# Router logits computed with the rows as matmul weights, the batch term put into the accumulator first, and the first rows and gate columns loaded and split in four slices by depth

## The chip, the cores and the metric

The kernel runs on one core of a Trainium2 chip. The metric is the device time of one execution in microseconds. The time before is the median of three runs.

The engines are TensorE (PE in the rows; its weight loads are shown apart as PEld), VectorE (DVE), ScalarE (ACT), GpSimd (POOL) and SyncE (SP). Each works through its own list of instructions in order and waits on semaphores; SyncE, ScalarE and GpSimd also issue DMA transfers. Products are summed in PSUM, which TensorE writes and VectorE and ScalarE read. All else lies in SBUF, with 128 partitions.

## What is computed

Two blocks over x of 32 batches x 128 rows x 512. The change touches the first part of the first block alone: a shared gated feed-forward and the router of eight routed experts. Cut to that:

```python
x_flat = x.reshape(N, C)                                   # N = 4096, C = 512
shared_out = einsum('nh,dh->nd', silu(x_flat @ sw1.T) * (x_flat @ sw3.T), sw2)   # 1024 hidden units
t_bias = t_emb @ router_t_w.T                              # one row of 8 per batch
s = sigmoid(x_flat @ router_w.T + t_bias_flat)             # N x 8
_, topk_idx = top_k(s + router_bias, 2)
...
```

The two best experts of each row then get gates, the routed experts run, a second feed-forward picks one expert for each batch, and the second block routes rows by a hash of their token and ends in a recurrence over 32 steps. None of that is changed.

## The kernel before

The program runs five stages one after the other: `stage_shared`, `stage_routed`, `stage_ffn`, `stage_hashed` and `stage_recurrent`. Most products are done in three parts: an operand is rounded to `float32r` (`_hi`, by ScalarE) and its remainder taken (`_lo`, by VectorE), and `product` (lines 95 to 101) issues hi x hi, lo x hi and hi x lo into one accumulator. The router logits are the exception: they are plain float32 matmuls, since they decide which experts are chosen.

`stage_shared` takes the 4096 rows in G = 8 groups of TG = 4 tiles of 128 rows, with the depth of 512 in DC = 4 slices of 128. For each group `gate_up(g, first, last)` makes HC = 8 chunks of 128 hidden units: 12 products for the gate, 12 for up, each with 128x128 weights and 512 columns (the rows of the group). ScalarE applies silu, VectorE multiplies (`hidden`), and `down(g)` makes the output.

The opening loads much at once. SyncE issues `x_raw`, the rows of group 0 transposed (1 MB, also the first half of `x_grp`), then four quarters of the weights, by `COLUMNS`: half 0 or 1 of the hidden units, layer 0 (gate) or 1 (up), 1 MB each. They land in buffers borrowed from others (`w_raw`, the second half of `x_grp`, `sg_h`). ScalarE first issues eleven small constants, then rounds x (`x_hi`, line 343) and each quarter (`split_columns`, line 354) as they land. VectorE follows with the remainders (`x_lo`, line 451, and line 457). TensorE waits for the last remainder that a chunk needs.

The router runs between the chunks of group 0. `score_t(g)` (line 730) makes the logits of one group turned round: weights `r_w[:, k]` of 8 columns, moving operand 512 columns of x, four float32 matmuls into an 8x512 accumulator. VectorE adds the batch term (`add_bias`, line 470) into `logits_sb`. `turn_scores(g)` (line 737) transposes the four tiles of 8x128 into `lg_ps`, whose layout is rows x experts x tiles. The batch term itself is made first of all (line 800). When the last group is there, ScalarE applies the sigmoid (line 374) behind the sixth chunk's silu, and VectorE starts its long chain: `choose`, `gates`, `slots`, `places`.

SyncE loads the rows of the later groups for the scores (`score_x`) into the two halves of `x_grp` in turn, a group ahead. A hash ranking also needs TensorE twice in this time, into `aux_ps` (lines 806 and 811): the product of ones with the memberships of the hashed experts, and that of a triangle with them, which waits until VectorE has copied the totals of the first (`hash_totals`, line 492). On VectorE `rank_weights` (line 511 on) makes small matrices for later ranks in `last_col` and others.

## Time and profile before

| | us |
|---|---|
| median of three runs | 2581.2 |
| lowest and highest | 2580.53, 2584.6 |
| profiled execution, its time | 2581.59 |
| its span in the trace | 2579.9 |
| mean granted clock of TensorE over the span | 0.986 |

The times of the rows are from the start of the span. Timeline rows give the start, the duration, the engine, the line, the operation, output <- inputs with their shapes, and in brackets how long the engine had stood idle and what ended that. A MATMUL row has a duration that includes its way through the array; successive products overlap, so the distance between two starts tells the pace. A float32 matmul stands in the rows as two MATMUL and two LDWEIGHTS entries. The granted clock is given as a share of the full 2.4 GHz. The first stretch of the page's table of slices has PE at 8 tenths and the next two at 9; what stands below about the opening comes from the timeline.

### The profile page before, as it was taken

To read this page: it belongs to the slowest core of one execution; us is meant where nothing else is said; L and a number is where in the kernel's file an instruction comes from. 1 tells how busy PE (TensorE), PEld (TensorE's weight loads), DVE (VectorE), ACT (ScalarE), POOL (GpSimd) and SP (SyncE) were. 2 spreads that over 40 slices of the span, in tenths; PEclk is the share of its full clock that TensorE was granted. 3 is DMA by queue.
4 is the path that set the end of the run, shared out by engine and by line. 5 is a ranking of instruction groups with operands and counts; after the bars stand their busy time and mean duration, and the time that the engine had idled before them with its cause. 6 is when DMAs were issued, how large, how long until landed. Compare 5 with 4: busy or idle time off the path is not lost. (4 is left out here: it accounts for less than half of the span.)

```text
span 2579.9 us, 40827 instructions
## 1 busy us (share of the span) xinstructions
PE 2482.1 (96%) x12552; PEld 2057.4 (80%) x12553; DVE 1146.0 (44%) x1756; ACT 901.3 (35%) x1446; POOL 552.3 (21%) x493
## 2 busy tenths in 40 slices
PE   8999999998989799999999989999989999999999
PEld 4778888887878578878888869989978888888876
DVE  5655555344422234434344346667643332333356
ACT  2233333235544312222222236666542222222233
POOL 1100000002222256657666610000001111111000
PEclk9999999999999899999999989999999999999999
DMA  7698898126474343363335356666641111111035
GB/s 288 216 338 308 304 329 314 71 110 208 139 267 137 108 156 109 114 252 108 118 104 190 98 194 237 230 230 228 230 153 33 33 33 29 29 33 33 16 107 170
DMA packets 134081, 413.05 MB, mean 160 GB/s; under 512 B 30082, under 2 KB 32578, under 8 KB 117872
## 3 DMA queue, kind: packets, MB, share of 16 engines
q1 hardware_dynamic: 106912, 317.61, 34.8%
q0 software_dynamic: 18736, 60.80, 7.8%
q10 hardware_dynamic: 8352, 33.60, 3.4%
q8 instruction: 46, 0.75, 0.1%
q14 instruction: 35, 0.29, 0.0%
HBM read 558.71 MB, written 144.80 MB: 273 GB/s over the span
## 5 line engine op out<-in xcount | busy, mean ns | idle before, releaser
L99 PE MATMUL s_g<-wx_hi,s_x_hi 128*128 128x512 f32 x512 | 207.0, 404 | 8.7 <-DVE s_x_lo L2093 4.2
L101 PE MATMUL s_g<-wx_hi,s_x_lo 128*128 128x512 f32 x512 | 202.0, 395 | 0.0
L100 PE MATMUL s_g<-wx_lo,s_x_hi 128*128 128x512 f32 x512 | 201.4, 393 | 0.0
L1840 DVE TENSOR_TENSOR s_w_lo<-s_w_raw,s_w_hi 128x1024 fp32r<-128x1024 f32 x124 | 146.5, 1223 | 76.3 <-ACT s_w_hi L1769 74.6
L99 PE MATMUL s_g<-s_u,s_c_hi 128*128 128x512 f32 x384 | 152.7, 398 | 1.6 <-PEq L1656 1.6
L101 PE MATMUL s_g<-s_u,s_c_lo 128*128 128x512 f32 x384 | 149.9, 390 | 0.0
L100 PE MATMUL s_g<-s_u,s_c_hi 128*128 128x512 f32 x384 | 149.5, 389 | 0.0
L99 PE MATMUL s_h_ps<-s_x_hi,s_w_hi 128*128 128x256 f32 x512 | 146.0, 285 | 1.5 <-DVE s_x_lo L1865 1.5
L100 PE MATMUL s_h_ps<-s_x_lo,s_w_hi 128*128 128x256 f32 x512 | 145.8, 285 | 0.0
L101 PE MATMUL s_h_ps<-s_x_hi,s_w_lo 128*128 128x256 f32 x512 | 145.8, 285 | 0.0
L2021 POOL DMA_INDIRECT s_y<-mid_hash_out,first_rec x32 | 31.7, 989 | 476.7 <-DMA mid_hash_out<-s_o 394.3
L99 PEld LDWEIGHTS s_g<-wx_hi,s_x_hi 128*128 128x128 f32 x512 | 97.2, 190 | 37.7 <-issue 9.2
L2104 DVE TENSOR_TENSOR s_gate<-s_g,s_bias 128x512 f32<-128x512 f32 x96 | 66.1, 691 | 136.9 <-PE s_g L101 136.9
L1769 ACT ACTIVATE s_w_hi<-s_w_raw 128x1024 fp32r<-128x1024 f32 x124 | 124.2, 1054 | 6.1 <-DMA s_w_raw<-in_w2h 6.1
L380 ACT ACTIVATE s_sg_h<-s_gate 128x512 f32<-128x512 f32 x64 | 38.4, 599 | 249.3 <-PE s_up L101 249.3
L2027 POOL TENSOR_TENSOR s_x<-s_y,s_r 128x512 f32<-128x512 f32 x32 | 44.2, 1381 | 365.6 <-ACT s_r L2039 355.5
L2051 ACT ACTIVATE s_gate<-s_gate 128x512 f32<-128x512 f32 x96 | 60.8, 634 | 176.0 <-DVE s_gate L2104 176.0
L634 DVE TENSOR_TENSOR s_sg_h<-s_sg_h,s_up 128x512 f32<-128x512 f32 x64 | 44.0, 688 | 170.0 <-ACT s_sg_h L380 169.8
L101 PEld LDWEIGHTS s_g<-wx_hi,s_x_lo 128*128 128x128 f32 x512 | 97.0, 190 | 21.5
L970 POOL DMA_INDIRECT s_x<-in_x_rows,route x68 | 67.0, 985 | 216.8 <-PE s_tx L1180 214.2
L99 PE MATMUL s_h_ps<-s_half,s_y_hi 128*128 x256 | 105.4, 412 | 7.1 <-DMA s_half<-mid_w 5.6
L100 PEld LDWEIGHTS s_g<-wx_lo,s_x_hi 128*128 128x128 f32 x512 | 97.2, 190 | 18.9
(372 smaller groups left out, 6778.9 us busy)
## 6 DMA issues: line engine op xcount, KB each, us to landing
s_half<-mid_w ACTq DMA_DIRECT2D x124, 2048.0 KB
s_half<-mid_w SPq DMA_DIRECT2D x20, 2048.0 KB
s_w_raw<-in_w SPq DMA_DIRECT2D x64, 512.0 KB, 6.2
mid_w<-s_x_grp SPq DMA_DIRECT2D x32, 1024.0 KB, 5.4
mid_w<-s_pool_b SPq DMA_DIRECT2D x32, 1024.0 KB, 4.9
s_w_raw<-in_w1h SPq DMA_DIRECT2D x16, 2048.0 KB, 7.5
s_w_raw<-in_w2h SPq DMA_DIRECT2D x16, 2048.0 KB, 7.5
mid_routed<-s_o_sb SPq DMA_DIRECT2D x72, 256.0 KB
```

Of the source, the lines that this page charges most:

```text
L99: pe.matmul(out, a_hi, w_hi, start=first, stop=False, skip_group_check=True)
L100: pe.matmul(out, a_hi, w_lo, start=False, stop=False, skip_group_check=True)
L101: return pe.matmul(out, a_lo, w_hi, start=False, stop=last, skip_group_check=True)
L380: act.activation(sg[:, c % 2], gate_ps[c % banks][:], ACT.Silu).then_inc(S["silu"], 1)
L634: dve.tensor_tensor(h[:, c % 2], sg[:, c % 2], up_ps[c % banks][:], ALU.mult).then_inc(S["hmul"], 1)
L970: pool.indirect_dma_start(x[:, i % NI], None, ins["x_rows"], bass.IndirectOffsetOnAxis(idx[:, i:i + 1].bitcast(U32), 0)).then_inc(E[f"tile ...
L1769: act.activation(hi[:, c], raw[:, c], ACT.Copy).then_inc(S[name + "_hi"], 1)
L1840: dve.tensor_tensor(lo[:, c], raw[:, c], hi[:, c], ALU.subtract).then_inc(S[name + "_lo"], 1)
L2021: pool.indirect_dma_start(y[:], None, d["hash_out"], bass.IndirectOffsetOnAxis(rec[:, SLOTH:SLOTH + 1].bitcast(U32), 0)).then_inc(S["y_in" ...
L2027: pool.tensor_tensor(x2[:], y[:], r[:], ALU.mult).then_inc(S["x2"], 1)
L2051: act.activation(gate[:, g], gate[:, g], f).then_inc(S["acted"], 1)
L2104: dve.tensor_tensor(gate[:, g], g_ps[n][g][:], bias[:, g], ALU.add).then_inc(S["added"], 1)
```

## The change

Four things are done.

1. **First slices.** x of group 0 and the first half of the gate weights are loaded as four slices each, by depth k: x slice, weight slice, x slice, and so on, each of 256 KB with a semaphore of its own. ScalarE and VectorE split them slice by slice (`split_first`). TensorE's first work is `first_chunks(2)`: the gate products of chunks 0 and 1, then their up products. In the first chunk it waits slice by slice.
2. **Constants.** Six of the eleven constants, those of the hash and the later ones, are issued by GpSimd instead of ScalarE.
3. **Logits.** `score(g)` uses each tile of x, 128x128, as the weights and `r_w[:, k]`, 8 columns, as the moving operand, and sums straight into `lg_ps`: 16 float32 matmuls a group. The transposes, `add_bias`, `logits_sb` and the two accumulators are gone.
4. **Batch term.** VectorE multiplies `rt_w` with `cond_t` for all depths, experts and batches (`bias_terms`, 1024 elements for each partition, in the buffer of `o_sb`). Four float32 matmuls with a matrix of ones as weights sum them over the partitions into `lg_ps`, before all scores. The ones lie in `last_col`, so `rank_weights` waits for the first scores.

The other changed numbers are semaphore counts that follow from this.

```diff
+        bias_terms = o_sb[:].rearrange("p a n -> p (a n)").rearrange("p (k e i) -> p k e i", k=DC, e=ER)
+        ones_32 = last_col
...
-            sp.dma_start(x_raw, ins["xt_groups"][0]).then_inc(S["xt_in"], 16)
-            for half, layer in COLUMNS:
+            for k in range(DC):
+                sp.dma_start(x_raw[:, :, k], ins["xt_groups"][0][:, :, k]).then_inc(S[f"first_x{k}"], 16)
+                sp.dma_start(columns[0][0][:, k], ins["sw"][k, :, 0:D]).then_inc(S[f"first_w{k}"], 16)
+            for half, layer in COLUMNS[1:]:
                 units = slice(layer * DC, (layer + 1) * DC)
                 if half and layer:
-                    sp.wait_ge(S["w_lo"], 2)
+                    sp.wait_ge(S["w_lo"], DC)
...
-                    sp.wait_ge(S["xt_lo"], 1)
-                wait_for(sp, S["logits_t"], g - 1)
+                    sp.wait_ge(S["xt_lo"], DC)
+                wait_for(sp, S["logits"], g - 1)
...
+            for dst, src, name in ((ids[:], ins["ids"], "hash_const"),
+                                   (expert_no, ins["c_expert"], "hash_const"), (new_run, ins["c_run"], "hash_const"),
+                                   (tile_no[:], ins["c_tile"], "late_const"), (token_no[:], ins["c_token"], "late_const"),
+                                   (r_bias[:], ins["r_bias"].partition_broadcast(P), "late_const")):
+                pool.dma_start(dst, src).then_inc(S[name], 16)
...
-                                   (ident[:], ins["c_ident"], "const"), (ids[:], ins["ids"], "hash_const"),
-                                   (expert_no, ins["c_expert"], "hash_const"), (new_run, ins["c_run"], "hash_const"),
-                                   (tile_no[:], ins["c_tile"], "late_const"), (token_no[:], ins["c_token"], "late_const"),
-                                   (r_bias[:], ins["r_bias"].partition_broadcast(P), "late_const")):
+                                   (ident[:], ins["c_ident"], "const")):
...
+            def split_first(k):
+                act.wait_ge(S[f"first_x{k}"], 16)
+                act.activation(xt_hi[:, :, k], x_raw[:, :, k], ACT.Copy).then_inc(S["xt_hi"], 1)
+                act.wait_ge(S[f"first_w{k}"], 16)
+                act.activation(w_hi[:, k, 0:D], columns[0][0][:, k], ACT.Copy).then_inc(S["w_hi"], 1)
...
-            x_hi(0)
-            for half, layer in COLUMNS:
+            for k in range(DC):
+                split_first(k)
+            for half, layer in COLUMNS[1:]:
...
+            def split_first(k):
+                dve.wait_ge(S["xt_hi"], k + 1)
+                dve.tensor_tensor(xt_lo[:, :, k], x_raw[:, :, k], xt_hi[:, :, k], ALU.subtract).then_inc(S["xt_lo"], 1)
+                dve.wait_ge(S["w_hi"], k + 1)
+                dve.tensor_tensor(w_lo[:, k, 0:D], columns[0][0][:, k], w_hi[:, k, 0:D], ALU.subtract).then_inc(S["w_lo"], 1)
...
-            def add_bias(g):
-                dve.wait_ge(S["logits_t"], g + 1)
-                wait_for(dve, S["logits"], g - 1)
-                dve.tensor_tensor(logits_sb[:, g % 2], score_ps[g % 2][0:ER],
-                                  batch_bias[:, g * TG:(g + 1) * TG, None].to_broadcast([ER, TG, P]),
-                                  ALU.add).then_inc(S["logits_sum"], 1)
...
                 last = ident[:, P - 1:P]
+                dve.wait_ge(S["logits"], 1)
                 op(dve.memset(last_col[:], 0.0))
...
-            x_lo(0)
-            split_columns(0, 0)
+            for k in range(DC):
+                split_first(k)
             split_columns(0, 1)
             dve.wait_ge(S["const"], 16 * n_const)
+            dve.memset(ones_32[:], 1.0).then_inc(S["bias_terms"], 1)
+            dve.tensor_tensor(bias_terms, rt_w[:, :, :, None].to_broadcast([P, DC, ER, NB]),
+                              cond_t[:, :, None, :].to_broadcast([P, DC, ER, NB]), ALU.mult).then_inc(S["bias_terms"], 1)
             dve.memset(ones[:], 1.0).then_inc(S["ones"], 1)
             dve.memset(ones_f[:], 1.0).then_inc(S["ones"], 1)
             dve.tensor_copy(tri[:], tri_f[:]).then_inc(S["ones"], 1)
-            dve.wait_ge(S["bias_ps"], 1)
-            signal(dve.tensor_copy(batch_bias[:], bias_ps), "bias")
-            add_bias(0)
             split_columns(1, 0)
             hash_members()
...
-            def score_t(g):
-                if g == 0:
-                    pe.wait_ge(S["xt_in"], 16)
-                else:
+            def bias_logits():
+                pe.wait_ge(S["bias_terms"], 2)
+                for k in range(DC):
+                    pe.matmul(lg_ps, ones_32[:], bias_terms[:, k], start=(k == 0), stop=False, skip_group_check=True)
+
+            def score(g):
+                if g:
                     pe.wait_ge(S[f"x_in{g % 2}"], (g + 1) // 2 * 16)
-                wait_for(pe, S["logits_sum"], g - 1)
-                for k in range(DC):
-                    mm = pe.matmul(score_ps[g % 2][0:ER], r_w[:, k], x_grp[:, g % 2, :, k], start=(k == 0),
-                                   stop=(k == DC - 1))
-                mm.then_inc(S["logits_t"], 1)
-
-            def turn_scores(g):
-                pe.wait_ge(S["logits_sum"], g + 1)
                 for tt in range(TG):
-                    mm = pe.transpose(lg_ps[:, :, g * TG + tt], logits_sb[:, g % 2, tt], ident[0:ER, 0:ER])
+                    for k in range(DC):
+                        mm = pe.matmul(lg_ps[:, :, g * TG + tt], x_grp[:, g % 2, tt, k], r_w[:, k], start=False,
+                                       stop=(k == DC - 1), skip_group_check=True)
                 mm.then_inc(S["logits"], 1)
+
+            def first_chunks(last):
+
+                for layer, outs in enumerate((gate_ps, up_ps)):
+                    if layer:
+                        pe.wait_ge(S["w_lo"], DC + 2)
+                    for c in range(last):
+                        for k in range(DC):
+                            if layer == 0 and c == 0:
+                                pe.wait_ge(S["xt_lo"], k + 1)
+                                pe.wait_ge(S["w_lo"], k + 1)
+                            w = slice(c * P, (c + 1) * P)
+                            u = layer * DC + k
+                            mm = product(pe, outs[c][:], (w_hi[:, u, w], w_lo[:, u, w]),
+                                         (xt_hi[:, :, k], xt_lo[:, :, k]), k == 0, k == DC - 1)
+                        if layer:
+                            mm.then_inc(S["gu"], 1)
...
+            first_chunks(NG0)
             pe.wait_ge(S["const"], 16 * n_const)
-            for k in range(DC):
-                mm = pe.matmul(bias_ps, rt_w[:, k], cond_t[:, k], start=(k == 0), stop=(k == DC - 1))
-            mm.then_inc(S["bias_ps"], 1)
-            score_t(0)
-            gate_up(0, 0, 1)
+            bias_logits()
+            score(0)
             pe.wait_ge(S["ones"], 3)
             pe.wait_ge(S["hash_members"], 1)
             pe.matmul(aux_ps[:, :], ones[:], flat, start=True, stop=True).then_inc(S["pe_rank"], 1)
-            gate_up(0, 1, 2)
-            score_t(1)
-            turn_scores(0)
+            score(1)
             pe.wait_ge(S["hash_total_read"], 1)
             pe.matmul(aux_ps[:, :], tri[:], flat, start=True, stop=True).then_inc(S["pe_rank"], 1)
             for c in range(2, 5):
                 gate_up(0, c, c + 1)
-                score_t(2 * c - 2)
-                turn_scores(2 * c - 3)
-                score_t(2 * c - 1)
-                turn_scores(2 * c - 2)
+                score(2 * c - 2)
+                score(2 * c - 1)
             gate_up(0, 5, 6)
-            turn_scores(G - 1)
             gate_up(0, 6, HC)
```

TensorE, between the second and the third chunk of group 0. `L730` is a score product (in the changed kernel `L735`), `L728` the batch term's sum, `s_first` holds `lg_ps`, `s_aux` the hash ranking. Before, with the end of chunk 1:

```order
L99 MATMUL s_up<-s_xt_hi,s_w_hi 128x512
L100 MATMUL s_up<-s_xt_lo,s_w_hi 128x512
L101 MATMUL s_up<-s_xt_hi,s_w_lo 128x512
L730 MATMUL s_up<-s_x_grp,s_r_w 8x512 x4
L737 MATMUL s_first<-ident,s_o_sb 128x8 x4
L811 MATMUL s_aux<-s_member,s_tri 128x512
L99 MATMUL s_gate<-s_xt_hi,s_w_hi 128x512
```

After:

```order
L99 MATMUL s_up<-s_xt_hi,s_w_hi 128x512
L100 MATMUL s_up<-s_xt_lo,s_w_hi 128x512
L101 MATMUL s_up<-s_xt_hi,s_w_lo 128x512
L728 MATMUL s_first<-s_o_sb,s_last_col 128x256 x4
L735 MATMUL s_first<-s_r_w,s_x_grp 128x8 x16
L820 MATMUL s_aux<-s_member,s_ones 128x512
L735 MATMUL s_first<-s_r_w,s_x_grp 128x8 x16
L823 MATMUL s_aux<-s_member,s_tri 128x512
L99 MATMUL s_gate<-s_xt_hi,s_w_hi 128x512
```

The scores of groups 0 and 1 and the batch term now stand together behind chunk 1; the ones product, which stood between chunk 0 and 1, follows the scores of group 0, and the transposes are gone.

VectorE, from its start to the first hash step. Line 451 is the remainder of x, line 457 that of the weights; in the changed kernel 464, 466 and 472. Before:

```order
L451 TENSOR_TENSOR s_xt_lo<-s_x_grp,s_xt_hi 128x2048 [waits s1_xt_hi]
L457 TENSOR_TENSOR s_w_lo<-s_w_raw,s_w_hi 128x2x512 [waits s1_w_hi] x2
L457 TENSOR_TENSOR s_w_lo<-s_x_grp,s_w_hi 128x2x512 [waits s1_w_hi] x2
L644 MEMSET s_ones 128x128 [waits s1_const]
L645 MEMSET s_ones_f 128x8
L646 CAST s_tri<-s_tri_f 128x128
L648 COPY s_batch_bias<-s_first 8x32 [waits s1_bias_ps]
L470 TENSOR_TENSOR s_o_sb<-s_gate,s_batch_bias 8x512 [waits s1_logits_t,s1_bias]
L457 TENSOR_TENSOR s_w_lo<-s_sg_h,s_w_hi 128x2x512 [waits s1_w_hi] x2
L481 TENSOR_SCALAR s_hash_id<-s_ids 128x32 [waits s1_hash_const]
```

After:

```order
L464 TENSOR_TENSOR s_xt_lo<-s_x_grp,s_xt_hi 128x4x128 [waits s1_xt_hi]
L466 TENSOR_TENSOR s_w_lo<-s_w_raw,s_w_hi 128x512 [waits s1_w_hi]
L464 TENSOR_TENSOR s_xt_lo<-s_x_grp,s_xt_hi 128x4x128 [waits s1_xt_hi]
L466 TENSOR_TENSOR s_w_lo<-s_w_raw,s_w_hi 128x512 [waits s1_w_hi]
L472 TENSOR_TENSOR s_w_lo<-s_x_grp,s_w_hi 128x2x512 [waits s1_w_hi] x2
L653 MEMSET s_last_col 128x128 [waits s1_const]
L654 TENSOR_TENSOR s_o_sb<-s_rt_w,s_cond_t 128x1024
L656 MEMSET s_ones 128x128
L657 MEMSET s_ones_f 128x8
L658 CAST s_tri<-s_tri_f 128x128
L472 TENSOR_TENSOR s_w_lo<-s_sg_h,s_w_hi 128x2x512 [waits s1_w_hi] x2
L489 TENSOR_SCALAR s_hash_id<-s_ids 128x32 [waits s1_hash_const]
```

The last two of the four slices stand at the head of the second piece (two more such pairs are ahead of it). The add of the batch term (`L470`) is gone, and the product `L654` of 1024 elements has come in front of the remainders of the third quarter.

SyncE, its first transfers. Before:

```order
L259 DMA s_x_grp<-in_xt_groups 128x2048
L264 DMA s_w_raw<-in_sw 128x4x512
L264 DMA s_x_grp<-in_sw 128x4x512
L264 DMA s_sg_h<-in_sw 128x4x512
L264 DMA s_w_raw<-in_sw 128x4x512 [waits s1_w_lo]
```

After:

```order
L258 DMA s_x_grp<-in_xt_groups 128x4x128
L259 DMA s_w_raw<-in_sw 128x512
L258 DMA s_x_grp<-in_xt_groups 128x4x128
L259 DMA s_w_raw<-in_sw 128x512
L258 DMA s_x_grp<-in_xt_groups 128x4x128
L259 DMA s_w_raw<-in_sw 128x512
L258 DMA s_x_grp<-in_xt_groups 128x4x128
L259 DMA s_w_raw<-in_sw 128x512
L264 DMA s_x_grp<-in_sw 128x4x512
L264 DMA s_sg_h<-in_sw 128x4x512
L264 DMA s_w_raw<-in_sw 128x4x512 [waits s1_w_lo]
```

Eight transfers stand where two stood, with the same bytes; the up columns (`s_x_grp<-in_sw`) come behind them.

## Rows read from the trace of the kernel before

**Rows 1.** The page: span, and busy time of the engines.
```profile
span 2579.9 us, 40827 instructions
...
PE 2482.1 (96%) x12552; PEld 2057.4 (80%) x12553; DVE 1146.0 (44%) x1756; ACT 901.3 (35%) x1446; POOL 552.3 (21%) x493
```

**Rows 2.** Stretches: start:end, length; busy us per engine, granted clock, DMA share, GB/s.
```profile
10.00:20.00 10.00, 9.97 (x33) 4.51 (x34) 9.86 (x12) 6.12 (x7) 0.00 (x0) 1.00 1.06 384
20.00:30.00 10.00, 8.89 (x37) 5.98 (x36) 7.88 (x21) 4.78 (x6) 0.00 (x0) 1.00 0.68 270
```

**Rows 3.** Timeline of the opening: start, us, engine, line, out<-in, idle before.
```profile
10.01 2.29 DVE L451 TENSOR_TENSOR s_xt_lo<-s_x_grp,s_xt_hi 128x2048 fp32r<-128x2048 f32 x1 [10.01 <-ACT s_xt_hi L343]
...
10.43 5.68 PE L730 MATMUL s_gate<-s_x_grp,s_r_w 128*8 128x512 f32 x8
...
13.44 2.00 ACT L354 ACTIVATE s_w_hi<-s_x_grp 128x1024 fp32r<-128x1024 f32 x2 [1.56 <-DMA s_x_grp<-in_sw]
...
14.53 2.36 DVE L457 TENSOR_TENSOR s_w_lo<-s_x_grp,s_w_hi 128x1024 fp32r<-128x1024 f32 x2
...
16.05 0.50 PE L99 MATMUL s_gate<-s_xt_hi,s_w_hi 128*128 128x512 f32 x1
...
22.94 0.38 PE L806 MATMUL s_aux<-s_member,s_ones 128*128 128x512 bf16 x1 [1.11 <-DVE s_member L488]
```

**Rows 4.** Timeline, VectorE, first step for the ranks and the copy of totals.
```profile
25.16 0.17 DVE L511 MEMSET s_last_col<- 128x128 f32 x1
...
27.31 0.68 DVE L492 COPY s_pool_b<-s_aux 128x512 f32<-128x512 f32 x1
```

**Rows 5.** Timeline, PE, the first product of the third chunk of group 0.
```profile
32.64 0.58 PE L99 MATMUL s_gate<-s_xt_hi,s_w_hi 128*128 128x512 f32 x1
```

**Rows 6.** DMA issues of the opening: KB, us from issue to landing.
```profile
s_x_grp<-in_sw SPq DMA_DIRECT2D x1, 1024.0 KB, 11.8
```

**Rows 7.** Timeline, PE, one pair of score groups and its neighbours.
```profile
51.48 0.39 PE L101 MATMUL s_up<-s_xt_hi,s_w_lo 128*128 128x512 f32 x1
51.80 3.60 PE L730 MATMUL s_gate<-s_x_grp,s_r_w 128*8 128x512 f32 x8
55.33 0.41 PE L737 MATMUL s_first<-ident,s_o_sb 8*128 8x8 f32 x4
...
59.54 0.50 PE L99 MATMUL s_gate<-s_xt_hi,s_w_hi 128*128 128x512 f32 x1
```

**Rows 8.** Timeline, four float32 matmuls of 128x128 weights and 32 columns.
```profile
662.85 0.97 PEld L1223 LDWEIGHTS s_th<-s_y_t,s_wp 128*128 128x128 f32 x8
...
663.74 0.19 PEld L99 LDWEIGHTS s_h<-s_w,s_x_hi 128*128 128x128 f32 x1
```

**Rows 9.** Timeline, ScalarE, behind the sixth chunk of group 0.
```profile
79.86 1.28 ACT L374 ACT_TABLE_LOAD   x1
```

**Rows 10.** Stretches with a long wait of PE, and one with transposes alone.
```profile
766.00:768.00 2.00, 0.00 (x0) 0.00 (x0) 0.00 (x0) 0.00 (x0) 0.00 (x0) 1.00 0.97 403
770.00:777.00 7.00, 0.00 (x0) 0.00 (x0) 0.04 (x1) 0.94 (x3) 0.00 (x0) 0.50 0.70 250
1522.00:1524.00 2.00, 1.75 (x8) 1.35 (x7) 0.43 (x1) 0.81 (x2) 0.00 (x0) 0.50 1.00 369
```

**Rows 11.** Timeline, weight loads of those transposes.
```profile
1521.79 1.56 PEld L1898 LDWEIGHTS s_tx_ps<-ident,s_x 128*128 128x128 f32 x8 [5.34 <-DMA s_x<-mid_hash_in]
```

**Rows 12.** Timeline, PE, the products after the wait of Rows 10.
```profile
777.53 0.79 PE L99 MATMUL s_o<-s_w,s_ht_hi 128*128 x1 [13.74 <-DVE s_ht_lo L1049]
778.11 0.63 PE L100 MATMUL s_o<-s_w,s_ht_hi 128*128 x1
778.54 0.63 PE L101 MATMUL s_o<-s_w,s_ht_lo 128*128 x1
...
783.65 0.39 PE L100 MATMUL s_o<-s_w,s_ht_hi 128*128 x1
783.88 0.39 PE L101 MATMUL s_o<-s_w,s_ht_lo 128*128 x1
```

43 lines of the change are left out of this document (16 added, 27 removed).

## The prediction, made before the changed kernel ran

> **What bounds the kernel now.** Start with the page: the profiled execution spans 2579.9 us, and PE is busy for 2482.1 us of it [rows 1]. A microsecond taken off TensorE's path, or put on it, therefore moves the end, unless another engine ends the stretch. The change touches only the first 80 us, the opening of `stage_shared`. So read the stretches next: from 10 us on PE is busy almost without a break, 9.97 of 10 us and then 8.89 of 10 [rows 2]. The idle part of the second stretch is one wait, 1.11 us in front of the product of ones with the hash memberships [rows 3]. Then ask what ends the wait of the first 16 us. The timeline shows PE working on `score_t(0)` from 10.43 us for 5.68 us [rows 3], while the first rows are rounded and their remainders taken; the first gate product starts at 16.05 us. The third chunk of group 0 starts at 32.64 us [rows 5]: that instant holds all that the opening costs, so I compare it before and after. After it, three pairs of score groups stand between chunks, in line on PE [rows 7].
>
> **A pair of score groups, before.** The last product ahead of the pair starts at 51.48, its successor would start 0.23 us later (the spacing in [rows 12] at the higher clock), and the first product behind the pair starts at 59.54 [rows 7]. The pair costs 59.54 - 51.48 - 0.23 = 7.83 us. Each group is 3.60 us of products, with 512 columns on 8-column weights, and 0.41 us of transposes, overlapping a little.
>
> **A pair, after.** Each group becomes 16 float32 matmuls whose weights are 128x128 rows and whose moving operand has 8 columns. A float32 matmul makes two weight loads in the trace, so a pair makes 64. The nearest row has the same weights and 32 columns: eight loads from 662.85 to the next load at 663.74 [rows 8], that is 0.89 / 8 = 0.111 us each. The moving part (32 columns) hardly counts there, so 8 columns shouldn't be slower or faster. 64 x 0.111 = 7.1 us, and I add 0.05 us for the change back to products: 7.15 us. Gain 0.68 us a pair, 2.0 us for three. Below, the bound is a load at the rate of the four transposes with 8-row data, about 0.41 / 4 = 0.1 us with the tail and some 0.07 without [rows 7]: 64 x 0.07 = 4.5 us a pair. Above, it is a load at the lower clock: eight loads in 1.56 us, 0.195 us each, in a stretch whose granted clock is 0.50, so 1.2 GHz [rows 10, 11]: 12.5 us a pair. I take 0.111, the row with the same weights and the full clock, and keep both ends. The transposes of the last group, behind the sixth chunk, disappear: 0.3 to 0.4 us, a gain of 0.35.
>
> **The opening, after.** The first gate chunk no longer waits for the whole of x and w, but the first up chunk still waits for all four depth slices of the up columns. These landed 11.8 us after their issue [rows 6]; ScalarE took them at 13.44 and VectorE was done with them at 14.53 + 2.36 = 16.89 us [rows 3]. Up to then the DMA engines ran at 384 GB/s, full [rows 2], and the bytes ahead of these columns are the same as before: the slices are cut from the same two transfers, and the constants only move from ScalarE's queue to GpSimd's. Nothing in the rows would bring the up columns sooner or later by more than about half a microsecond. So up to 16.9 us PE has only the two gate chunks, 24 products. The fourth slice lands at about 9.5 us (2.1 MB of slices and some constants at 384 GB/s after 2.5 us); ScalarE and VectorE need about 0.5 and 0.6 us for a 512-element piece (a quarter of 2.29 us, a quarter of 2.36 us [rows 3]), so its products can start between 10.6 and 12.2 us. Fifteen products are then left: 15 x 0.43 = 6.5 us at the lower clock, 15 x 0.23 = 3.5 us at the higher [rows 12]. A mix of 5 us ends them at 15.6 to 17.2 us. The gate chunks hide in the wait for the up columns, just so.
>
> From 16.9 us: 24 up products x 0.23 = 5.5; the bias, four matmuls of 256 columns where 512 columns cost 3.60 [rows 7], so 1.8; score(0), 3.55; the ones product 0.2; score(1), 3.55; the tri product 0.2; changes between kinds 0.2. Sum 15.0, so the third chunk starts at 31.9 instead of 32.64 us [rows 5]: a gain of 0.7 us. That is little, although 5.68 us of `score_t(0)` and 1.11 us of waiting [rows 3] leave the path: score(0) now stands in the stream, and the bias is dearer than the 0.6 us that it was in idle time.
>
> **The waits that the change adds.** On VectorE the first memset for the ranks, at 25.16 us before, now waits for score(0), because the ones of the bias share its buffer. Queued behind it are the other rank operations, `hidden(0,0)` and the copy of the totals, which before were through at 27.31 + 0.68 = 27.99 us, so 2.8 us behind the memset [rows 4]. PE wants the totals for the tri product. It gets there 0.2 + 3.55 = 3.75 us after score(0): a cover of about 0.9 us. If it is gone, the wait costs what is missing, under 1 us. On SyncE the loads of the second and later groups now wait for the scores themselves; a megabyte lands in 5 to 7 us and is wanted a chunk and a score group later, 9 us: costed at nothing, and 1 to 2 us at once if the DMA engines are full there. The bias terms, one operation of 1024 elements, 1.2 us by half of 2.36 [rows 3], and the later constants on VectorE lie beside the up products. Everything behind the sixth chunk hangs on the sigmoid of the logits, whose table load starts at 79.86 us [rows 9] right behind that chunk's work on ScalarE, so VectorE's long chain on the chosen experts moves with PE and takes nothing of the gain.
>
> **Sum.** 2.0 + 0.35 + 0.7 = 3.1 us. The profiled execution took 2581.6 us, 0.4 above the median of 2581.2, so 2581.6 - 3.1 = 2578.5 us: 0.12% less, inside the 0.2% (5.2 us) that a measurement of this kernel can tell from no change.
>
> **Rival 1, the clock falls under the scores (slower).** A pair of score groups leaves the array with 8 columns per load for 7.1 us. In this trace the granted clock goes to 0.50 (1.2 GHz) after PE has had nothing to do: PE waited from 763.8 us, the clock was 1.00 at 766 to 768 us and 0.50 from 770 us [rows 10, 12]. It comes back some 5 us after products resume; until then they start 0.43 us apart instead of 0.23 [rows 12]. If loads with few columns weigh as idleness, each of the four stretches of scores (the first two groups, three pairs) runs some 4 us at full speed and 3.1 us of work at half, +3.1 us, and the next chunk spends 5 us at half, +2.5 us: 5.6 x 4 = 22 us, so 2578.5 + 22 = 2601 us. If only the products slow and the loads don't, 2.5 x 4 = 10 us, 2588 us. Two falls are enough to end slower than before by over 0.2%. For it: no stretch of the trace with full clock has so few columns for over 1 us. Against it: the loads keep the engine busy without a gap, and the clock stayed at 1.00 everywhere before where PE had no gap.
> [...]
>
> **Rival 2, cheap loads (faster).** If a load with 8 columns goes at 0.07 us, a pair takes 4.5 us and each of the first two groups 2.2: 3 x 2.65 + 2 x 1.3 = 10.5 us more, less about 1 us of wait for the totals: 2569 us. Against it stands the row with 32 columns, whose columns already take a small part.
>
> **Rival 3, the opening gives nothing back or takes.** Slices in short pieces and constants on GpSimd's queue arrive late, or PE meets the up chunks at the lower clock: the third chunk then starts at 33 to 35 us, and the time is 2579.5 to 2581.5 us. That is the case in which the slices don't do what they are cut for. It is inside "same" and part of the forecast's own range.
>
> **Chances and range.** Forecast with rival 3: 0.52, of which 0.08 lies below 2576.0 (loads or opening a little better). Rival 1: 0.37, half near 2601 or above, half between 2584 and 2598. Rival 2: 0.07. Other slowdowns, such as a late group of rows in the scores: 0.04, half of it over 0.2%. Faster 0.08 + 0.07 = 0.15; slower 0.37 + 0.02 = 0.39; same 0.46. From 2575 to 2603 us about 0.17 is left out: most of rival 2 below, the upper end of rival 1 above. The likeliest case alone would have 2575.5 to 2582 us.
>
> **What would show it.** In the timeline of PE: the first gate product at 7 to 8 us and the first up product at 16.9; score(0) behind them; the third chunk of group 0 at 31.9; loads of the scores 0.11 us apart, and a pair in 7.1 to 7.2 us. A granted clock below 1.00 between 24 and 80 us shows rival 1; loads under 0.08 us apart show rival 2; a start of the third chunk after 33 us shows rival 3. The sum is wrong if the part behind 80 us isn't shifted as a whole, which the start of the sigmoid's table load against the end of the sixth chunk would tell.

## The result: slower by 1.25%

| | before | changed |
|---|---|---|
| median on one chip (us) | 2582.0 | 2616.0 |
| lowest and highest (us) | 2580.5, 2584.6 | 2612.0, 2618.2 |
| profiled execution, its time (us) | 2581.59 | 2615.57 |
| its span (us) | 2579.9 | 2613.9 |
| mean granted clock | 0.986 | 0.975 |

The ratio is 1.0125, with a 95% interval of 1.0112 to 1.0138. The change costs 32 to 34 us. The forecast was 2578.5 us, and the range ended at 2603: the time lies above both. One execution of the experiment e4_few took 5837 us and is left out of its ratio; why it did isn't known.

From the page of the changed kernel, the span and the busy time of each engine (before: [rows 1]):

```profile
span 2613.9 us, 41147 instructions
...
PE 2510.9 (96%) x12712; PEld 2105.9 (81%) x12713; DVE 1142.4 (44%) x1754; ACT 901.2 (34%) x1451; POOL 556.0 (21%) x499
```

PE is busy for 28.8 us more than before. So TensorE isn't waiting for something new over most of the loss: it works longer on the same chunks. The windows of the changed kernel say why (columns: busy time and count of PE, PEld, DVE, ACT, POOL, then the granted clock, DMA share, GB/s):

```profile
20.00:30.00 10.00, 10.00 (x56) 8.45 (x54) 8.81 (x18) 6.33 (x7) 0.00 (x0) 1.00 0.43 155
30.00:40.00 10.00, 10.00 (x53) 9.57 (x53) 3.81 (x11) 0.63 (x1) 0.00 (x0) 0.60 0.65 226
...
50.00:60.00 10.00, 10.00 (x40) 9.19 (x40) 3.26 (x9) 0.00 (x0) 0.00 (x0) 0.53 0.88 279
60.00:70.00 10.00, 10.00 (x61) 9.44 (x59) 3.65 (x4) 3.01 (x4) 3.20 (x6) 0.81 0.56 183
70.00:80.00 10.00, 10.00 (x35) 8.70 (x35) 0.00 (x0) 0.00 (x0) 0.00 (x0) 0.51 0.82 315
...
90.00:100.00 10.00, 10.00 (x35) 8.37 (x36) 0.00 (x0) 0.08 (x1) 0.00 (x0) 0.66 0.23 92
100.00:110.00 10.00, 10.00 (x46) 8.29 (x45) 8.14 (x16) 5.12 (x7) 6.41 (x12) 1.00 0.73 243
```

PE is busy for 10 of 10 us in each, yet from about 32 to 97 us the clock is partly at half, 1.2 GHz. In the kernel before PE is just as busy there, and the clock is 1.00:

```profile
30.00:60.00 30.00, 30.00 (x109) 13.87 (x108) 14.52 (x24) 4.12 (x6) 7.01 (x13) 1.00 0.69 238
60.00:90.00 30.00, 30.00 (x125) 19.82 (x124) 14.18 (x24) 8.20 (x11) 10.15 (x19) 1.00 0.76 273
```

TensorE's timeline in the changed kernel gives the milestones: the third chunk of group 0 at 38.01 (32.64 before, [rows 5]), a pair of score groups from 45.71 to 56.13, and the first product of the output of group 0, `down(0)`, at 110.60 and of group 1, `down(1)`, at 183.59.

```profile
38.01 0.99 PE L99 MATMUL s_gate<-s_xt_hi,s_w_hi 128*128 128x512 f32 x1
```

```profile
45.71 0.51 PE L735 MATMUL s_first<-s_r_w,s_x_grp 128*128 128x8 f32 x4
```

```profile
56.13 0.77 PE L99 MATMUL s_gate<-s_xt_hi,s_w_hi 128*128 128x512 f32 x1
```

```profile
110.60 0.40 PE L99 MATMUL s_first<-s_d_hi,s_ht_hi 128*128 128x512 f32 x1
```

```profile
183.59 0.40 PE L99 MATMUL s_first<-s_d_hi,s_ht_hi 128*128 128x512 f32 x1
```

In the kernel before `down(0)` starts at 89.97 and `down(1)` at 157.98 us. The ledger of the shift, changed minus before:

| stretch | before | changed | shift | forecast |
|---|---|---|---|---|
| start to third chunk | 32.64 | 38.01 | +5.4 | -0.7 |
| third chunk to `down(0)` | 57.33 | 72.59 | +15.3 | -2.35 |
| `down(0)` to `down(1)` | 68.01 | 72.99 | +5.0 | 0 |
| `down(1)` to the end | 2421.9 | 2430.3 | +8.4 | 0 |

The second row splits by the starts of chunks and pairs: the three pairs take 10.42, 10.78 and 9.50 us instead of 7.74 each (+7.5), the three chunks ahead of them 7.70, 7.06 and 8.30 instead of some 5.7 (+6.0), and the last three chunks +1.8.

### The profile page after: what moved, and what is told of

Its sections match the earlier page's. It is cut to its first block and busy times, and to the rows that moved or that the text cites. A ratio compares the mean times of both kernels' runs of the same rounds, so it can differ in the third digit from the quotient of the medians.

```text
span 2613.9 us, 41147 instructions
## 1 busy us (share of the span) xinstructions
PE 2510.9 (96%) x12712; PEld 2105.9 (81%) x12713; DVE 1142.4 (44%) x1754; ACT 901.2 (34%) x1451; POOL 556.0 (21%) x499
## 5 line engine op out<-in xcount | busy, mean ns | idle before, releaser
L99 PE MATMUL s_gate<-s_xt_hi,s_w_hi 128*128 128x512 f32 x256 | 107.0, 418 | 15.9 <-DVE s_w_lo L466 11.1
```

Of the source, the lines that this page charges most:

```text
L99: pe.matmul(out, a_hi, w_hi, start=first, stop=False, skip_group_check=True)
```

## Experiments

Each kernel is told as its difference from the changed kernel unless said otherwise. Ratios are to the kernel before on the same chip, whose median was between 2581.5 and 2585.9 us. The changed kernel itself wasn't run again on the chips of the experiments, so a comparison of two ratios from different chips may hold something of the chips too. Each `down` instant is from one profiled execution.

| run | ratio | 95% interval | `down(0)` | `down(1)` |
|---|---|---|---|---|
| changed kernel | 1.0125 | 1.0112 to 1.0138 | 110.6 | 183.6 |
| e1_whole | 1.0106 | 1.0086 to 1.0126 | 112.1 | 180.9 |
| e2_slices | 1.0017 | 1.0008 to 1.0027 | 93.8 | 162.1 |
| e3_spread | 1.0230 | 1.0213 to 1.0248 | 138.5 | 208.7 |
| e4_few | 1.0014 | 1.0004 to 1.0024 | 91.1 | 159.8 |
| e5_wide64 | 1.0032 | 1.0021 to 1.0043 | 90.7 | 165.3 |
| e6_wide128 | 1.0035 | 1.0023 to 1.0048 | 90.3 | 163.0 |
| e7_pad | 1.0095 | 1.0078 to 1.0111 | 112.3 | 185.3 |
| e8_consts | 1.0088 | 1.0071 to 1.0105 | 109.3 | 180.1 |
| e9_idle | 1.0023 | 1.0012 to 1.0034 | 91.0 | 161.6 |
| e10_idle_rec | 1.0018 | 1.0009 to 1.0026 | 92.1 | 157.9 |
| e11_x_whole (one run, 2610.5 us) | | | 108.7 | 181.1 |
| e12_w_whole (one run, 2616.6 us) | | | 111.2 | 183.3 |
| e13_before_rec | 1.0000 | 0.9989 to 1.0010 | 90.3 | 156.2 |
| e14_fill3_rec | 0.9994 | 0.9985 to 1.0003 | 88.4 | 154.3 |
| e15_after_rec | 1.0114 | 1.0096 to 1.0132 | 111.0 | 177.3 |

### Is it the scores or the loads? (e1, e2, e4)

e1_whole undoes the loading, e2_slices keeps only the loading.

```diff
 e1_whole
-            for k in range(DC):
-                sp.dma_start(x_raw[:, :, k], ins["xt_groups"][0][:, :, k]).then_inc(S[f"first_x{k}"], 16)
-                sp.dma_start(columns[0][0][:, k], ins["sw"][k, :, 0:D]).then_inc(S[f"first_w{k}"], 16)
+            sp.dma_start(x_raw, ins["xt_groups"][0]).then_inc(S["first_x0"], 16)
+            sp.dma_start(columns[0][0], ins["sw"][0:DC, :, 0:D].rearrange("u p n -> p u n")).then_inc(S["first_w0"], 16)
```

> The changed kernel with the loading of before: x of group 0 and the first gate columns whole, all eleven constants issued by ScalarE; the new logits and the order of TensorE stay. Theory A (thin work lowers the clock, the opening is a smaller part): TensorE starts the gate products at about 16 us as before, and 48 products (11.1 us), the bias (1.9) and two score groups (7.4) put the third chunk at 36.5 to 37 us, against 38.0 in the changed kernel and 32.6 before; the granted clock falls to about a half in the same places; the time is 2608 to 2616 us. Theory B (the late, sliced loads shift everything and the clock falls for the shifts alone): with the loads as before the clock stays at 1.00 up to 110 us and the time is 2583 to 2588 us.

> The kernel before with only the loading changed: four slices of x and of the gate columns, six constants on GpSimd's queue; the logits, their bias and TensorE's order are those of before. Theory A: the up columns land 3 to 4 us later as in the changed kernel, their products start at about 20.6 us instead of about 18.7, the third chunk starts at 34 to 36.5 us, the clock stays at 1.00 from 20 to 110 us, and the time is 2584 to 2590 us. Theory B: the clock falls between 30 and 90 us here too and the time is 2600 us or more.

e1_whole: 2610.2 us, a ratio of 1.0106. e2_slices: 2587.1 us, 1.0017, with TensorE in the order of before. The clock tells them apart. The first fence has windows of e2_slices, with all of `score_t` and the transposes in them, the second those of e1_whole:

```profile
30.00:60.00 30.00, 30.00 (x111) 14.77 (x110) 15.27 (x27) 5.24 (x8) 6.96 (x13) 1.00 0.67 234
60.00:90.00 30.00, 30.00 (x120) 17.86 (x119) 11.99 (x20) 8.20 (x11) 8.05 (x16) 1.00 0.77 277
```

```profile
30.00:40.00 10.00, 10.00 (x63) 9.88 (x63) 3.81 (x11) 0.63 (x1) 0.00 (x0) 0.68 0.55 211
...
50.00:60.00 10.00, 10.00 (x46) 9.52 (x46) 4.66 (x11) 0.00 (x0) 1.45 (x3) 0.53 0.88 278
...
70.00:80.00 10.00, 10.00 (x38) 9.03 (x38) 0.00 (x0) 0.00 (x0) 0.00 (x0) 0.50 0.94 346
```

The sliced loading alone costs 0.17%, some 4.4 us, and leaves the clock alone. It costs more in the old order than was expected there (the up products at 22.58 us, not 20.6): TensorE's first work, `score_t(0)`, needs all four slices of x and starts at 14.22 us, where whole rows let it start at 10.43. The new logits with the old loading keep the low clock and about 27 us of the loss. Theory B is out. In e1_whole the third chunk came at 39.5 us, 2.5 later than expected: the clock fell under score(1) there too, which the expectation had left out of that instant. The old loading doesn't bring the new order forward either: the first up product starts at 22.27 us in e1_whole and at 20.61 in the changed kernel.

In e4_few each of the groups 2 to 7 makes one of its 16 score matmuls.

```diff
-                for tt in range(TG):
-                    for k in range(DC):
+                for tt in range(TG if g < 2 else 1):
+                    for k in range(DC if g < 2 else 1):
```

> The changed kernel with the scores of groups 2 to 7 cut to one of their sixteen matmuls each, so that the logits of these groups lack most of their sum. Theory A: without thin stretches the clock stays at 1.00 from about 42 us on; the third to eighth chunk take 6 x 5.5 us from 38.0 us and down(0) can start at about 72 us, 38 us earlier than in the changed kernel, if VectorE's chain lets it; the time is 2576 to 2588 us. Theory B (the clock falls whatever the scores do): low stretches stay where they were and only the scores' own 21.5 us go at most, 2592 to 2597 us.

2586.5 us. The time is as theory A has it, but the instant wasn't: `down(0)` started at 91.1 us, not 72. What the scores no longer took, TensorE spent waiting for the later groups' rows, as the list of PE's waits between 40 and 90 us shows (us in total, times, longest):

```profile
PE s_first L735 <- DMA s_x_grp<-in_xt_groups: 11.1, 3, 4.4
```

So this run doesn't price the scores cleanly; it shows that a megabyte of rows for each group is the next limit of the stretch, close behind. The waits let the clock fall too (0.64 to 0.84 between 50 and 80 us), so the run doesn't show by its clock that the scores lowered it.

### What of the scores lowers the clock? (e3, e5, e6)

e3_spread issues the score tiles of groups 2 to 7 one by one between the products of chunks 2 to 4.

```diff
+                            if tiles is not None:
+                                score_tile(tiles + layer, k)
...
-                gate_up(0, c, c + 1)
-                score(2 * c - 2)
-                score(2 * c - 1)
+                gate_up(0, c, c + 1, tiles=2 * c - 2)
```

> The changed kernel, but the 24 score tiles of groups 2 to 7 are issued one by one, each behind a twelfth of... that is behind each three products of chunks 2, 3 and 4, eight tiles to a chunk, instead of eight in a row behind the chunk. Theory A1 (what counts is how long TensorE has nothing but thin work, some 7 us at once): the clock is 1.00 from 45 to 90 us, down(0) starts 12 us earlier than at 110.6, and the time is 2598 to 2604 us. Theory A2 (what counts is the share of thin work, in whatever order): the clock falls as it did, down(0) starts within 2 us of 110.6, and the time is 2612 to 2618 us.

2641.4 us, 1.0230: worse than either expectation. The clock didn't recover between the tiles at all (windows of e3_spread):

```profile
40.00:60.00 20.00, 20.00 (x75) 17.97 (x74) 0.00 (x0) 0.00 (x0) 0.00 (x0) 0.50 0.23 85
60.00:80.00 20.00, 20.00 (x77) 18.16 (x76) 6.67 (x13) 1.11 (x2) 3.77 (x7) 0.50 0.43 144
...
100.00:120.00 20.00, 20.00 (x76) 18.21 (x75) 1.16 (x2) 1.79 (x3) 1.53 (x3) 0.50 0.03 9
```

In the changed kernel the runs of plain products between the pairs brought the clock back each time; mixed in, the same thin work held it at 1.2 GHz for more than 80 us (some of them waiting for rows). The clock was already at half when the mixing began at 38.96 us. So the run shows that thin work in short pieces, between products, is enough to keep the clock from coming back; whether it would also bring it down from 1.00 wasn't tried.

e5_wide64 and e6_wide128 keep every load and every matmul in its place, and only widen the moving side. `r_w` stands in a zeroed field with a step of WI between its columns, so that a window of 8 x WI columns puts it at its tile and adds zeros to the neighbours'.

```diff
-                        mm = pe.matmul(lg_ps[:, :, g * TG + tt], x_grp[:, g % 2, tt, k], r_w[:, k], start=False,
+                    b, o = divmod(g * TG + tt, WI)
+                        mm = pe.matmul(lg_ps[:, :, b * WI:(b + 1) * WI], x_grp[:, g % 2, tt, k],
+                                       window(k, o), start=False,
```

> The changed kernel, but the moving operand of each score matmul has 64 columns: r_w stands in a field of zeros, and a window of it puts the 8 columns at the place of their tile, so that a matmul adds zeros to seven other tiles' columns. The number of matmuls and loads, their weights and their order stay. Theory C (the clock falls because few columns stream through the array for each load): the share of low clock between 30 and 110 us shrinks or is gone, the time lies between 2595 and 2612 us. Theory D (it is the float32 loads of 128x128 one behind another, whatever streams): the clock falls as before and the time is 2614 to 2620 us.

> As the one with 64 columns, with 128. By the row of 512 columns (3.60 us for eight passes, 0.45 us each) a pass of 128 takes 0.11 us, as long as a load. Theory C: the clock is 1.00 from 20 to 110 us, a pair takes 7.2 to 8 us instead of 10.4, down(0) starts at 94 to 98 us instead of 110.6, and the time is 2592 to 2600 us; if the column passes don't lie beside the loads, a pair takes 14 us at full clock and the time is about 2620 us with a clock of 1.00. Theory D: the clock falls in the same places, 2614 to 2620 us.

Both end at 2595 us, 1.0032 and 1.0035, some 0.9% less than the changed kernel's ratio. Windows of e5_wide64, and then the loads of both first score groups in e6_wide128:

```profile
30.00:40.00 10.00, 9.95 (x71) 9.24 (x72) 3.81 (x11) 0.63 (x1) 0.00 (x0) 1.00 0.67 260
40.00:60.00 20.00, 20.00 (x150) 18.75 (x149) 10.34 (x17) 4.12 (x6) 6.95 (x13) 1.00 0.83 295
60.00:80.00 20.00, 19.81 (x125) 17.50 (x125) 3.65 (x4) 3.01 (x4) 3.72 (x7) 1.00 0.85 312
```

```profile
27.99 3.76 PEld L746 LDWEIGHTS s_first<-s_scratch,s_x_grp 128*128 128x128 f32 x32
...
31.77 3.76 PEld L746 LDWEIGHTS s_first<-s_scratch,s_x_grp 128*128 128x128 f32 x32
```

The clock stays at 1.00 and the 32 loads take 3.76 us in both groups, 0.117 us each, just as the 8-column loads at full clock. In the changed kernel the second group of the same loads took 6.59 us:

```profile
27.74 3.76 PEld L735 LDWEIGHTS s_first<-s_r_w,s_x_grp 128*128 128x128 f32 x32
...
31.44 6.59 PEld L735 LDWEIGHTS s_first<-s_r_w,s_x_grp 128*128 128x128 f32 x32
```

Theory C holds and D is out: at the same loads, the same operands as weights and the same busy share of the engine, the number of columns that stream decides, though the added ones carry zeros. Nothing between 8 and 64 was tried. 64 are enough here, and 128 cost no more than 64, since their passes lie beside the loads: a pair takes 7.06 us in both (41.45 to 48.51 in e5_wide64), a little under the 7.15 that the prediction had for full clock. `down(0)` came at 90.3 us in e6_wide128, earlier than the 94 to 98 expected. What is left of the loss in e5_wide64 isn't in the scores: by `down(0)` it is 0.7 us behind the kernel before, by `down(1)` 7.3, with a wait of TensorE of 5.1 us between them (below).

### The addresses and the constants (e7, e8)

```diff
 e7_pad
+        pad = sb("pad", [ER, NB])
         scratch = sb("scratch", [P, 3, ER * NB])
```

> The changed kernel with an unused buffer of the size of batch_bias (128 bytes for each partition) in its old place, so that all buffers behind it have the addresses of before. Theory E (the removal of batch_bias moved ht_hi and its neighbours, and at the new addresses the products of down run 0.233 us apart instead of 0.229): a first half of down takes 5.50 us instead of 5.60 as in the run with only the slices, 32 such pieces give back 3.2 us, and the time is 2611 to 2614 us. Rival F (the slower pace of down comes from the new logits or the clock): 5.60 us stay, 2615 to 2617 us.

The fences have the third and fourth pieces of `down(0)` in the changed kernel and in e7_pad, each the first product of a piece:

```profile
122.14 0.39 PE L99 MATMUL s_first<-s_d_hi,s_ht_hi 128*128 128x512 f32 x1
...
127.74 0.39 PE L99 MATMUL s_aux<-s_d_hi,s_ht_hi 128*128 128x512 f32 x1
```

```profile
123.58 0.39 PE L99 MATMUL s_first<-s_d_hi,s_ht_hi 128*128 128x512 f32 x1
...
129.08 0.40 PE L99 MATMUL s_aux<-s_d_hi,s_ht_hi 128*128 128x512 f32 x1
```

5.60 against 5.50 us, 5.50 also in every other kernel that has the 128 bytes (before, e2, e9, e10, e13, e14) and 5.60 in every one that has not. Theory E holds: 32 such pieces are 3.2 us of the loss, and it belongs to where `ht_hi`, `ht_lo` and their neighbours lie, not to the logits. Why those addresses are slower isn't settled. The whole time doesn't test it: e7_pad's ratio lies 0.30%, 7.8 us, under the changed kernel's, more than twice the 3.2 us, while its `down(1)` comes 1.7 us later. The other 4.6 us aren't explained, and may be the chip's.

e8_consts issues all eleven constants from ScalarE again.

```diff
 gpsimd
-            for dst, src, name in ((ids[:], ins["ids"], "hash_const"),
...
-                pool.dma_start(dst, src).then_inc(S[name], 16)
 scalar
-                                   (ident[:], ins["c_ident"], "const")):
+                                   (ident[:], ins["c_ident"], "const"), (ids[:], ins["ids"], "hash_const"),
```

> The changed kernel with all eleven constants issued by ScalarE as before; the slices stay. Theory G (the six constants on GpSimd's queue take DMA time from the slices in the first 8 us): the last slice of x is taken by ScalarE 1 to 2 us earlier than at 13.7 us, the up columns' products start at 18.5 to 19.5 us instead of 20.6, and the third chunk at 36 to 37 us instead of 38.0; the time is 2614 us. Rival H (it is the slices themselves, eight issues on one queue ahead of the up columns' load and short pieces): the up products start at 20 us or later and the time is 2615 to 2618 us, or more since ScalarE issues eleven constants before it splits.

The up products started at 21.06 us, not earlier than the 20.61 of the changed kernel: rival H, the constants on GpSimd's queue aren't what delays the opening. The time, 2607.8 us, was lower than both expectations, a ratio 0.37% (9.5 us) under the changed kernel's, with intervals that don't touch. Of that only 3.5 us are seen by `down(1)` (180.1 against 183.6); the rest lies behind it and isn't explained.

### The opening (e11, e12)

```diff
 e11_x_whole
+            sp.dma_start(x_raw, ins["xt_groups"][0]).then_inc(S["first_x0"], 16)
             for k in range(DC):
-                sp.dma_start(x_raw[:, :, k], ins["xt_groups"][0][:, :, k]).then_inc(S[f"first_x{k}"], 16)
 e12_w_whole
-                sp.dma_start(columns[0][0][:, k], ins["sw"][k, :, 0:D]).then_inc(S[f"first_w{k}"], 16)
+                if k == 0:
+                    sp.dma_start(columns[0][0], ins["sw"][0:DC, :, 0:D].rearrange("u p n -> p u n")).then_inc(S["first_w0"], 16)
```

> The changed kernel with x of group 0 in one transfer and the gate columns still in four slices. Theory K (the pieces of 512 bytes of the x slices are slow): ScalarE takes the up columns at 13.5 to 14.5 us as before instead of 17.1, TensorE starts the up products at 17 to 18.5 us, the third chunk at 35 to 36 us. Rival L (more issues on SyncE's queue, each about 0.6 us, put the up columns back): the up columns are issued at 4.5 to 6 us and taken at 15 to 16 us. Rival M (slices of the weights too are slow): 16.5 us or later.

> The changed kernel with the gate columns in one transfer and x of group 0 still in four slices. Theory K: the up columns are taken at 16.5 us or later, as late as in the changed kernel, since the pieces of 512 bytes stay. Rivals L and M: at 15 to 16 us, half of the delay gone, or less.

ScalarE takes the up columns at these times in e11_x_whole and e12_w_whole:

```profile
16.81 2.01 ACT L362 ACTIVATE s_w_hi<-s_x_grp 128x1024 fp32r<-128x1024 f32 x2 [3.03 <-DMA s_x_grp<-in_sw]
```

```profile
16.56 2.00 ACT L363 ACTIVATE s_w_hi<-s_x_grp 128x1024 fp32r<-128x1024 f32 x2 [1.27 <-DMA s_x_grp<-in_sw]
```

Before it was 13.44 [rows 3], in the changed kernel 17.10. Slicing only the weights delays them by 3.4 us and slicing only the rows by 3.1, so each kind of slice brings nearly the whole delay: e11_x_whole came out as rival M has it and e12_w_whole as theory K. The place on the queue isn't it. In e11_x_whole the load of the up columns was issued at 3.29 us, in the changed kernel at 7.48, and it was used only 0.3 us earlier. The rate of the first 10 us is lower with either kind, 260 GB/s in e11_x_whole and 253 in e12_w_whole (294 before, 219 in the changed kernel). Each of the two ran once; what in a slice does it stays open. The third chunk came at 36.28 and 38.43 us. What the runs do show is that no variant with slices had the up columns before 16.5 us, and each one with whole transfers had them at 13.4 to 13.9 us.

### The 5 us between the first two `down` (e10, e13, e15)

In the changed kernel TensorE waits 4.8 us before one gate product of group 1 (1.9 before), and ScalarE has waited for a load of an expert weight:

```profile
PE s_gate L99 <- DVE s_sg_h L643: 4.8, 1, 4.8
```

```profile
145.33 1.06 ACT L375 ACTIVATE s_x_grp<-s_w_raw 128x1024 fp32r<-128x1024 f32 x1 [11.19 <-DMA s_w_raw<-in_w]
```

GpSimd had issued the store of `rec`, 96 KB in tiny pieces, at 127.84 us. The first fence has its row in the list of DMA issues (KB, us to landing), the second the window behind it:

```profile
mid_rec<-s_rec POOLq DMA_DIRECT2D x1, 96.0 KB, 14.6
```

```profile
130.00:140.00 10.00, 10.00 (x46) 8.14 (x45) 2.13 (x2) 0.66 (x2) 0.00 (x0) 1.00 1.03 88
```

It takes 14.6 us to land, and the DMA engines are busy all the time and move only 88 GB/s. The load of `s_w_raw` issued at 133.63 us is behind it and is used only at 145.33. ScalarE's list is in order, so the silu of the next chunk waits too. VectorE waits for the same piece, to 146.42 us, and has 6.3 us of routing operations in its list behind it before the product that TensorE needs, at 153.90. The test holds the store back to the seventh group:

```diff
             pool.wait_ge(S["rec_done"], 1)
+            pool.wait_ge(S["gu"], 6 * HC + 4)
             pool.dma_start(d["rec"].rearrange("i p c -> p i c"), rec[:]).then_inc(S["rec_out"], 16)
```

e15_after_rec is the changed kernel with it, e13_before_rec the kernel before with it. e9_idle and e10_idle_rec are the version described in their expectations, without and with it; in those two the batch term begins a second sum in the bank that holds group 0's scores, so the logits lack part of group 0, and the rows go to other experts than in the rest of the runs. Their whole times are therefore weak evidence; the instants up to `down(1)` are used here.

> The changed kernel with the store of rec put back in the same way. Theory I: the wait of 4.8 us of PE on s_sg_h near 150 us is gone and with it the fall of the clock behind it; from down(0) to down(1) it takes 66 to 67 us instead of 73.0 (110.60 to 183.59), and the time is 5 to 7 us less than that of the changed kernel, a ratio of 1.0095 to 1.011. Rival (the wait has another cause): ratio 1.0115 to 1.0135.

> The kernel before with nothing changed but the store of rec, which GpSimd issues only after the fifth chunk of the seventh group instead of at 106.7 us. Theory I (the store holds up the weight load behind which ScalarE stands): the wait of 1.9 us on s_sg_h and those of 0.5 to 1 us behind it between 120 and 165 us are gone, down(1) starts at 155.5 to 156.5 us instead of 158.0, the time is 2 to 2.5 us less, a ratio of 0.9988 to 0.9995. Rival: the store collides with something as dear later on, 0.9995 to 1.0005.

> As e9_idle, but GpSimd stores rec (the 96 KB in 14.5 us of DMA time, issued around 107 us) only after the fifth chunk of the seventh group. Theory I (that store holds up the expert-weight load behind which ScalarE stands, and so makes TensorE wait 1.9 to 5.1 us for a product between 120 and 160 us): the wait of PE on s_sg_h between chunks of group 1 is gone or under 0.5 us, ScalarE takes its piece less than 4 us late, and down(1) starts 2 to 5 us earlier than in e9_idle, counted from down(0); the time is 2 to 5 us less. Rival J (the load is late for another reason, its buffer or the stream of other loads): the wait stays at 2 us or more and the time is that of e9_idle within 1 us.

From `down(0)` to `down(1)` it takes 66.3 us in e15 (73.0 in the changed kernel), 65.9 in e13 (68.0 before), 65.9 in e10 (70.7 in e9), and PE's waits on `s_sg_h` are gone in all three. In e15 the same load, issued at 133.26 us, is used at 137.90, and the clock stays at 1.00 from 110 to 200 us, where it fell to 0.50 behind the wait in the changed kernel. Theory I holds. The two fences have `down(1)` in e15 and in e13:

```profile
177.33 0.40 PE L99 MATMUL s_first<-s_d_hi,s_ht_hi 128*128 128x512 f32 x1
```

```profile
156.17 0.39 PE L99 MATMUL s_first<-s_d_hi,s_ht_hi 128*128 128x512 f32 x1
```

e10 takes 2586.9 us where e9 takes 2589.5, and their intervals overlap. On the whole time the gain isn't to be seen elsewhere either: e13's ratio is 1.0000 (0.9989 to 1.0010) where 0.9988 to 0.9995 was expected, e15's 1.0114, between the 1.0095 to 1.011 of theory I and the rival's 1.0115 to 1.0135, overlaps the changed kernel's interval. What is gained by 160 us can be lost again later; where, the runs don't tell.

### A version with all of it put right (e9, e14)

```diff
 e9_idle, from e5_wide64 with the loads of e1_whole and the pad of e7_pad
-            first_chunks(NG0)
             pe.wait_ge(S["const"], 16 * n_const)
-            bias_logits()
+            pe.wait_ge(S["first_x0"], 16)
             score(0)
+            bias_logits()
+            first_chunks(NG0)
```

> The version that the runs so far point to: the new logits with the 64-column window, the loading of before (whole transfers, constants from ScalarE), the address pad, the scores of group 0 first and the batch term behind them, both in the wait for the first gate columns (terms multiplied by GpSimd), and the product of ones behind the second chunk. If the clock stays at 1.00 as with 64 columns before, a pair costs 7.06 us where it was 7.83 (3 x 0.77 = 2.3 us), the last and the first turning go (0.35 each), the 1.11 us of waiting for the hash memberships go, and the fill of the wait ends near the 16.05 us of before: the third chunk starts at 31 to 32 us, down(0) at 86 to 87 us instead of 90.0, and the ratio to the kernel before is 0.9975 to 1.0. If the fill overruns the wait (terms late on GpSimd), the third chunk starts at 33 to 35 us and the ratio is 1.000 to 1.001. Rival: with thin work in the slow first microseconds the clock falls once, +5 us, 1.002.

e9_idle missed: the third chunk came at 35.9 us, `down(0)` at 91.0 instead of 86 to 87, and the ratio was 1.0023. TensorE was busy with the scores (10.47 to 17.32 us) and the batch term until the first gate product at 21.04 us instead of 16.05, while VectorE had its operands ready at 16.67. So the fill was longer than the wait. Beside it, two engines got in each other's way. The first fence has VectorE in e9_idle, the second GpSimd:

```profile
10.36 4.04 DVE L473 TENSOR_TENSOR s_xt_lo<-s_x_grp,s_xt_hi 128x2048 fp32r<-128x2048 f32 x1 [10.36 <-ACT s_xt_hi L364]
```

```profile
10.35 1.90 POOL L325 TENSOR_TENSOR s_o_sb<-s_rt_w,s_cond_t 128x1024 f32<-128x1024 f32 x1
```

While GpSimd multiplied the bias terms, VectorE's subtraction of x, 2.29 us before [rows 3], took 4.04 us. The Trainium skill, "GPSIMD Engine Reference", section "Specifications", says that the two engines share their SBUF interface and contend when a VectorE instruction has two SBUF inputs; the subtraction has two, and this row agrees. In e10_idle_rec VectorE started 0.08 us ahead of GpSimd and not behind it:

```profile
10.16 2.29 DVE L474 TENSOR_TENSOR s_xt_lo<-s_x_grp,s_xt_hi 128x2048 fp32r<-128x2048 f32 x1 [10.16 <-ACT s_xt_hi L365]
12.37 4.07 DVE L477 TENSOR_TENSOR s_w_lo<-s_w_raw,s_w_hi 128x1024 fp32r<-128x1024 f32 x2
```

```profile
10.24 3.98 POOL L325 TENSOR_TENSOR s_o_sb<-s_rt_w,s_cond_t 128x1024 f32<-128x1024 f32 x1
```

Now VectorE's subtraction has its 2.29 us and GpSimd's 1.90 us become 3.98; VectorE's next two operations take 4.07 us instead of 2.35 and end at 16.44. The times fit engines that take turns by whole operations, the one that starts first going ahead at its full pace.

> e10_idle_rec with a smaller fill and a cheaper batch term: three tiles of group 0 are scored in the wait for the first gate columns (24 loads x 0.21 us at the lower clock = 5.1 us, as long as the 5.68 us of score_t(0) in the kernel before), the fourth behind the first two chunks; VectorE sums the bias terms over depth first, so that one matmul of 256 columns (0.45 us) remains of four. Expected by theory: gate products from 16.1 us, third chunk at 32.3 to 33 us, 0.77 us saved for each of three pairs and 0.35 for the last turning, the store of rec out of the way (2.1 us): down(1) at 153 to 154.5 us instead of 158.0, the ratio to the kernel before 0.998 to 0.9988. Rival: the opening takes back what the pairs give (VectorE later by its two sums, the fill again longer than the wait): third chunk at 34 us or later and the ratio 0.999 to 1.0.

```diff
 e14_fill3_rec, from e10_idle_rec
-            score(0)
-            bias_logits()
+            score(0, 0, 3)
             first_chunks(NG0)
+            bias_logits()
+            score(0, 3)
 vector
+            dve.tensor_tensor(bias_terms[:, 0:2], bias_terms[:, 0:2], bias_terms[:, 2:4], ALU.add).then_inc(S["bias_terms"], 1)
+            dve.tensor_tensor(bias_terms[:, 0], bias_terms[:, 0], bias_terms[:, 1], ALU.add).then_inc(S["bias_terms"], 1)
```

VectorE multiplies the bias terms again, and only the first score matmul of all starts the bank anew, so the logits are whole.

e14_fill3_rec, from TensorE's timeline: three tiles in the wait, one matmul for the batch term, then the rest of the scores.

```profile
10.47 5.35 PE L750 MATMUL s_first<-s_scratch,s_x_grp 128*128 128x64 f32 x24 [10.47 <-POOL s_scratch L323]
...
28.60 0.59 PE L739 MATMUL s_first<-s_o_sb,s_last_col 128*128 128x256 f32 x2
29.03 4.74 PE L750 MATMUL s_first<-s_scratch,s_x_grp 128*128 128x64 f32 x40
33.60 0.38 PE L842 MATMUL s_aux<-s_member,s_tri 128*128 128x512 bf16 x1
```

`down(0)` comes at 88.4 and `down(1)` at 154.3 us, 1.6 and 3.7 earlier than in the kernel before, the second as expected (153 to 154.5); the third chunk, at 33.6, was 1 us later than before and missed the 32.3 to 33. The time is 2578.6 us against 2581.5, a ratio of 0.9994 with an interval of 0.9985 to 1.0003. The forecast of 0.998 to 0.9988 failed; the ratio is where the rival had it. That is no gain that these runs can tell from none. By `down(1)` it is 1.9 us ahead of e13_before_rec, which has the same late store: so much the scores as weights and the cheaper batch term are worth here.

## Why the prediction was wrong

- **A pair of score groups, 0.111 us a load: right as a price, wrong as a forecast.** At full clock the loads take 0.117 us (3.76 / 32) and a pair 7.06 us, in e5_wide64. The row with 32 columns [rows 8] was a fair price for the load. But it was 0.89 us long, and said nothing of what 7 us of such work do to the clock. The prediction took the full clock since "the loads keep the engine busy without a gap". That is the step that failed: in the changed kernel PE is busy 10 of 10 us at a clock of 0.51 to 0.53, and the three pairs take 10.42, 10.78 and 9.50 us where 7.15 was forecast. The reckoning of this stretch was right for the full clock: in e5_wide64 the third chunk starts at 35.77 us and `down(0)` at 90.69, 54.9 us apart, 2.4 less than before, and -2.35 was forecast.
- **Rival 1 was what happened.** It had 5.6 us for each of four stretches, 22 us in all. Measured: +2.8 us in the second score group (6.32 us where 3.55 was forecast), and +15.3 instead of -2.35 up to `down(0)`, 17.6 us: together 20. By `down(0)` e5_wide64 is 19.9 us ahead of the changed kernel; its ratio is 0.93% lower, 24 us. Size and mechanism were right; the chance of 0.37 was too low, for the argument against it was an assumption about what the clock looks at.
- **The opening, -0.7 forecast, +5.4 measured.** Of the difference of 6.1 us, 3.7 were there at the first up product (20.61 us for 16.9). The other 2.4 are the clock under the second group less some small terms. The 3.7 have two causes, each enough alone. One stands against "nothing in the rows would bring the up columns sooner or later by more than about half a microsecond". SyncE's queue in the changed kernel:

```profile
5.78 1.66 SPq L259 DMA_DIRECT2D s_w_raw<-in_sw  x1
7.48 0.44 SPq L264 DMA_DIRECT2D s_x_grp<-in_sw  x1
```

  The load of the up columns was the third on the queue before, issued at 1.62 us; now it is the ninth, issued at 7.48. In the first 10 us the DMA engines moved 219 GB/s where they had moved 294. The prediction counted the bytes ahead of the columns and took the rate as 384 GB/s, which [rows 2] has for the second 10 us only. The later issue doesn't matter by itself (e11_x_whole). The slices themselves were late as well:

```profile
6.82 0.76 PE L99 MATMUL s_gate<-s_xt_hi,s_w_hi 128*128 128x512 f32 x1 [6.82 <-DVE s_w_lo L466]
...
11.72 0.77 PE L99 MATMUL s_gate<-s_xt_hi,s_w_hi 128*128 128x512 f32 x1 [3.29 <-DVE s_w_lo L466]
...
15.89 0.76 PE L99 MATMUL s_gate<-s_xt_hi,s_w_hi 128*128 128x512 f32 x1
```

  The first product came at 6.82 us, about as forecast (7 to 8), the fourth slice's at 15.89 instead of 10.6 to 12.2. So the two gate chunks filled the time to 20.6 us in which the up columns were also not ready, and the first up product came at 20.61 instead of 16.9. From there to the third chunk 15.0 us were forecast, and at full clock that is what it takes: 14.6 us in e5_wide64 (21.14 to 35.77). Rival 3 had this mechanism, with 35 us as its upper end: too little.
- **The waits on VectorE and SyncE cost nothing: right.** The memset for the ranks waited 2.6 us, to 31.68, but the copy of the totals was through at 34.51, before TensorE's tri product at 37.98; at full clock it would still have been 0.7 us ahead (31.66 + 3.55 = 35.21).
- **The part behind 80 us moves as a whole: right up to `down(0)`, wrong behind it.** The sigmoid's table load came right behind the sixth chunk's silu, at 101.06 us. But from `down(0)` on the kernel is not a rigid block: the store of `rec` met the weight load at a worse phase (+4.6 of the +5.0: it costs 6.7 us there in the changed kernel and 2.1 before), and 128 bytes fewer in SBUF put 3.2 us on `down`. Neither had a term or a rival. Of the +8.4 us behind `down(1)` 2.8 are the addresses; the other 5.6 were not traced to a cause. What a kernel gained or lost there against the kernel before went from -3.8 us (e14) to +8.9 (e9), so single profiles don't settle it.
- **The range** ended at 2603 since it held Rival 1 alone. From the forecast to the 2615.6 us of the profiled execution it is 37 us: the clock 20, the late first up product 3.7, the store 4.6, the addresses 3.2, and the 5.6 that weren't traced.

## What to carry to other kernels

Don't let TensorE's busy time stand for its clock: before you turn a wide matmul into one with few moving columns, ask how long a stretch has few columns, and if it can't be avoided try to widen the moving side with zeros, which is free as far as the columns pass beside the load. When loads are cut into pieces, look up when the next transfer on the same queue lands: here it came 3 us later with either kind of piece. Buffers removed or moved shift the addresses of all behind them; keep a pad in place when an edit is to be measured by itself.

## What the runs showed of the hardware

- Back-to-back float32 loads of 128x128 with 8 moving columns brought the granted clock to its lower level (1.2 GHz), although PE had no gap (31.44: 6.59 us for the same 32 loads as 3.76); with 64 or 128 columns it stayed at 1.00. Once it was down, three products of 512 columns in turn with eight such loads kept it at 0.50 from 40 to 80 us, again with PE busy without a gap. The Trainium skill, "TensorE: Matmul & The Clock Gate", section "Why this matters for your kernels", lays drops of the clock in the middle of a kernel to gaps in which TensorE is idle. One fall in the changed kernel agrees: PE waited 4.8 us, to 154.65, and the clock was 0.50 from 156 to 158 us. The falls under the scores don't: they came without a gap.
- A load under the low clock took 0.195 us (e3_spread, eight loads from 38.96 to the next product at 40.52), as [rows 11] had it, and 0.21 in the slow first microseconds of e14 (24 loads from 10.47 to 15.59). There the granted clock is recorded as 1.00, but the pace is that of the lower level.
- A 128-byte shift of the buffers changed the pace of `down` from 5.50 to 5.60 us for 24 products.
- One 96 KB store in small pieces kept the DMA engines busy at 88 GB/s and put another queue's 512 KB load back to 11.7 us from issue to use (133.63 to 145.33); with the store out of the way it was 4.6 us (133.26 to 137.90, e15).
- VectorE's 2048-element subtraction took 4.04 us instead of 2.29 beside a GpSimd multiplication of 1.90 us (e9); where VectorE had started first, it took its 2.29 and the multiplication 3.98 (e10).
